# Gated edges on one Trainium2 core: sums written into the gathered rows (four buffers), loads by pairs, and a new wait before every second gather

## The reference, cut to what matters

```
concat   = [h[src], h[dst], edge_attr]            # 96 + 96 + 64 values for each edge
gates    = sigmoid(concat @ W_e + b_e)
messages = softplus(concat @ W_n + b_n)
h_new    = segment_sum(gates * messages, dst)
x        = x + h + h_new / max(edge_count, 1)
```

## Time and profile before

| | us |
|---|---|
| three runs | 3172.36, 3173.5, 3178.24 (median 3173.5) |
| the profiled execution, its own time | 3187.08 |
| its span, first to last instruction | 3185.3 |
| gated_edges within the span, about | 1266 to 2562 |

### The profile page before, as it was taken

The page is one execution under the profiler, slowest core; times in us unless marked ns, Lnnn a source line. Parts: engine busy times, 40 slices in busy tenths (PEclk is TensorE's granted clock), DMA queues, the critical chain, the costliest instruction groups (busy, mean ns, idle before and its releaser), DMA issues. The chain is left out here.

```text
span 3185.3 us, 64234 instructions
## 1 busy us (share of the span) xinstructions
PE 2435.4 (76%) x20386; PEld 2294.3 (72%) x20387; DVE 1740.3 (55%) x3596; ACT 1347.9 (42%) x2794; POOL 922.5 (29%) x1144
## 2 busy tenths in 40 slices
PE   3888889869999997665666656666566669859999
PEld 2877778759999996565566655666556557649999
DVE  7877787773444435554555445554455452345555
ACT  2544445433333332444444444444444420207776
POOL 2112111200000000566566666666666600000000
PEclk7999999979999998555555555555555559878999
DMA  2333333320000002333333333333333360028272
GB/s 67 117 101 101 104 115 103 100 77 2 2 2 2 2 2 86 95 90 91 90 91 94 91 91 89 91 93 91 90 90 91 88 244 22 1 88 348 93 259 78
DMA packets 203915, 284.20 MB, mean 89 GB/s; under 512 B 88387, under 2 KB 169542, under 8 KB 198310
## 3 DMA queue, kind: packets, MB, share of 16 engines
q1 hardware_dynamic: 164806, 201.09, 19.4%
q0 software_dynamic: 38880, 79.68, 9.6%
HBM read 211.08 MB, written 69.57 MB: 88 GB/s over the span
## 5 line engine op out<-in xcount | busy, mean ns | idle before, releaser
L1105 POOL DMA_INDIRECT layer_R<-source_terms,layer_srcs x804 | 785.4, 977 | 486.4 <-DVE layer_zp L1151 261.9
L1318 PE MATMUL layer_zp<-layer_right,layer_left 96*128 96x192 f32 x1350 | 471.7, 534 | 496.9 <-DVE layer_left L1123 472.3
L1318 PEld LDWEIGHTS layer_zp<-layer_right,layer_left 96*128 96x128 f32 x1350 | 403.3, 324 | 514.9 <-DVE layer_left L1123 474.9
L540 PE MATMUL build_win<-nodes_x,build_S 128*128 128x200 bf16 x5264 | 501.7, 252 | 126.5 <-DVE nodes_x L457 121.9
L540 PEld LDWEIGHTS build_win<-nodes_x,build_S 128*128 128x128 bf16 x5264 | 442.4, 99 | 182.0 <-DVE nodes_x L457 117.2
L910 PEld LDWEIGHTS layer_acc<-layer_U,graph_CT 128*128 128x128 f16 x6250 | 517.0, 98 | 26.5 <-issue 22.7
L910 PE MATMUL layer_acc<-layer_U,graph_CT 128*128 128x192 f16 x6250 | 521.1, 246 | 19.0 <-DVEq L759 19.0
L1151 DVE TENSOR_TENSOR layer_zp<-layer_zp,layer_R 128x1152 f32<-128x1152 f32 x135 | 184.4, 1366 | 370.7 <-remote 368.8
L1267 ACT ACTIVATE layer_y<-layer_zp 128x1152 f32<-128x1152 f32 x135 | 152.6, 1130 | 445.9 <-DVE layer_zp L1151 445.2
L1339 PEld LDWEIGHTS layer_acc<-layer_hot,layer_G 128*98 128x98 f32 x1644 | 289.0, 274 | 9.3 <-issue 3.4
L1836 PE MATMUL layer_acc<-layer_V,layer_turn 128*128 128x96 f32 x2500 | 288.6, 278 | 0.6 <-issue 0.6
(11 more groups left out here) (240 smaller groups left out, 2825.4 us busy)
## 6 DMA issues: line engine op xcount, KB each, us to landing
layer_ring<-W_blocks SPq DMA_DIRECT2D x41, 1600.0 KB, 7.7
W_blocks<-nodes_x SPq DMA_DIRECT2D x400, 100.0 KB, 1.8
layer_left<-in_attr SPq DMA_DIRECT2D x135, 192.0 KB
C_blocks<-build_Cblk SPq DMA_DIRECT2D x25, 800.0 KB, 3.6
layer_C<-C_blocks SPq DMA_DIRECT2D x25, 800.0 KB, 22.0
layer_R<-source_terms,layer_srcs POOLq DMA_INDIRECT x804
layer_rows<-target_rows SPq DMA_DIRECT2D x135, 48.0 KB
layer_right<-target_terms SPq DMA_DIRECT2D x135, 24.0 KB
```

The lines of the kernel that those rows point to most:

```text
L540: mm = pe.matmul(out, S[:, b, part, 2 * i + u, :, :].rearrange("p a z -> p (a z)"), M[:, i, u, :, :].rearrange("p a z -> p (a z)"), start= ...
L1105: nc.gpsimd.indirect_dma_start(R[:, h, u, :], None, P_d, bass.IndirectOffsetOnAxis(ap=at_u, axis=0)).then_inc(s_R[h], 16)
L1318: pe.matmul(out[u], left[:, h, u * P:(u + 1) * P], right[:, h, :], start=(u % 2 == 0), stop=False, skip_group_check=True)
```

## The change

`left`, `right`, `rows` and `R` get four buffers each (i = s % LONG); `zp`, `z`, `y`, `G` and `hot` keep two. The add writes its sum into `R[:, i]`, and the absolute value and the logs read it there. PE's product of step s then waits for the add of step s-2 in place of the logs of step s-2. The turned one-hots are made two steps ahead. SP loads for two steps at once, with one semaphore for each pair of buffers, after the product of step s-3. POOL no longer waits for the add of step s-2; it waits for the logs of step s-4 (the last readers of the buffer it fills), and in an even step also for the product of that same step. (`s_z` now begins at 4, so a count of s + 5 means that the product of step s is done.)

```
-        left = m.sb("left", [DK, 2, SE * P], F32)
-        right = m.sb("right", [DK, 2, D2], F32)
+        left = m.sb("left", [DK, LONG, SE * P], F32)
+        right = m.sb("right", [DK, LONG, D2], F32)
-        rows = m.sb("rows", [DK, 2, SE * P], I16)
-        R = m.sb("R", [P, 2, SE, D2], F32)
+        rows = m.sb("rows", [DK, LONG, SE * P], I16)
+        R = m.sb("R", [P, LONG, SE, D2], F32)
...
+            def loads(j, s):
+                two = slice(2 * j, 2 * j + 2)
+                edges = bass.ds(s * (SE * P), 2 * SE * P)
+                sp.wait_ge(s_z, s + 2)
+                sp.sem_inc(s_taken, 1)
+                sp.dma_start(rows[DE:DK, two, :].rearrange("p i e -> p (i e)"),
+                             row_d[:, edges].to_broadcast([QW, 2 * SE * P])).then_inc(s_pair[j], 16)
+                sp.dma_start(left[0:DE, two, :].rearrange("p i e -> p (i e)"), attr[:, edges]).then_inc(s_pair[j], 16)
+                for i in range(2 * j, 2 * j + 2):
+                    sp.dma_start(right[DE:DK, i, :], Q_d[bass.ds(step_base(sp, bases[i]), QW), :]).then_inc(s_pair[j], 16)
...
             for s in range(NS):
-                h = s % 2
+                i = s % LONG
                 if s == 1:
                     pool.wait_ge(s_srcs, 16)
-                pool.wait_ge(s_add, s + 1)
+                if s >= LONG - 1:
+                    pool.wait_ge(s_ms, s)
+                if s >= 2 and s % 2 == 0:
+                    pool.wait_ge(s_z, s + 5)
...
-            def turned(h, s, pair):
-                dve.wait_ge(s_rows[h], pair * 16 + 16)
+            def turned(i, s, turn):
+                if i % 2 == 0:
+                    dve.wait_ge(s_pair[i // 2], turn * 64 + 64)
...
-            def add(h, s, pair):
-                dve.wait_ge(s_R[h], (pair * 16 + 16) * SE)
-                dve.wait_ge(s_z, s + 3)
-                nc.vector.tensor_tensor(zp[h][:, :, 0:D2], zp[h][:, :, 0:D2], R[:, h, :, :], ALU.add).then_inc(s_add, 1)
+            def add(h, i, s, turn):
+                dve.wait_ge(s_R[i], (turn * 16 + 16) * SE)
+                dve.wait_ge(s_z, s + 5)
+                nc.vector.tensor_tensor(R[:, i, :, :], zp[h][:, :, 0:D2], R[:, i, :, :], ALU.add).then_inc(s_add, 1)
-            def logs(h, s):
+            def logs(h, i, s):
                 dve.wait_ge(s_l, s + 2)
-                nc.vector.scalar_tensor_tensor(z[:, h, :, D:], zp[h][:, :, D:D2], 0.0, y[:, h, :, D:],
+                nc.vector.scalar_tensor_tensor(z[:, h, :, D:], R[:, i, :, D:D2], 0.0, y[:, h, :, D:],
                                                ALU.max, ALU.add)
...
-                logs(1 - h, s - 1)
-                add(h, s, pair)
+                logs(1 - h, (i - 1) % LONG, s - 1)
+                add(h, i, s, turn)
                 if not last:
-                    turned(1 - h, s + 1, pair + h)
+                    turned((i + 2) % LONG, s + 2, turn + i // 2)
...
-                nc.scalar.activation(y[:, h, :, :], zp[h][:, :, 0:D2], ACT.Abs).then_inc(s_abs, 1)
+                nc.scalar.activation(y[:, h, :, :], R[:, i, :, :], ACT.Abs).then_inc(s_abs, 1)
...
-                pe.wait_ge(s_ms, s + 2)
-                pe.wait_ge(s_at[h], pair * 16 + 16)
+                pe.wait_ge(s_add, s + 1)
+                if i % 2 == 0:
+                    pe.wait_ge(s_pair[i // 2], turn * 64 + 64)
                 pe.wait_ge(s_hT, s + 3)
-                pe.wait_ge(s_Qs[h], pair * 16 + 16)
```

More of the change, by code:

```diff
@@ L996, in gated_edges @@
         s_init = m.sem("buffers_set")
[L997 to L1000, removed]
+        s_pair = [m.sem(f"two_steps_loaded{j}") for j in range(2)]
+        s_R = [m.sem(f"source_terms_gathered{i}") for i in range(LONG)]
         s_taken = m.sem("waits_taken")
@@ L1083, in loads @@
                         sp.dma_start(rightx[DE:DK, :], Q_d[bass.ds(past(b, v), QW), :]).then_inc(s_xQ, 16)
[L1085 to L1089, removed]
+            with sp.Fori(0, NL) as four:
+                four_steps(sp, bases, counts, four)
+                for j in range(2):
+                    loads(j, four * LONG + 2 * j)
+                    for i in range(2 * j, 2 * j + 2):
+                        more_loads(i)
         @block.gpsimd
@@ L1190, in accumulate, with step @@
                         dve.sem_inc(s_taken, 1)
-            def step(i, s, turn, pair, last):
+            def step(i, s, turn, last):
                 h = i % 2
@@ L1208, in step @@
                 onehots(h, s)
-            for words in (zp[1][:, :, 0:D2], gate, z[:, :, :, :], y[:, :, :, :], G[:, :, :, 0:D + 1], hot[:, :, :, :],
+            for words in (R[:, LONG - 1, :, :], gate, z[:, :, :, :], y[:, :, :, :], G[:, :, :, 0:D + 1], hot[:, :, :, :],
                           leftx[:, :], rightx[0:DE, :]):
@@ L1228, in _ @@
             turned(0, 0, 0)
+            turned(1, 1, 0)
             with dve.Fori(0, NS // LONG) as four:
                 for i in range(LONG):
-                    step(i, four * LONG + i, four, four * (LONG // 2) + i // 2, False)
+                    step(i, four * LONG + i, four, False)
             for s in range(NS // LONG * LONG, NS):
-                step(s % LONG, s, s // LONG, s // 2, s == NS - 1)
+                step(s % LONG, s, s // LONG, s >= NS - 2)
             gated(1, NS - 2)
-            logs(0, NS - 1)
+            logs(0, (NS - 1) % LONG, NS - 1)
             accumulate(1, NS - 2, bases[(NS - 2) % LONG], counts[(NS - 2) % LONG])
@@ L1281, in _ @@
                 for i in range(LONG):
-                    step(i % 2, four * LONG + i)
+                    step(i, four * LONG + i)
             for s in range(NS // LONG * LONG, NS):
-                step(s % 2, s)
+                step(s % LONG, s)
             gates(0, NS - 1)
@@ L1300, in _ @@
             pe.wait_ge(s_init, 1)
-            pe.wait_ge(s_wa, 80)
+            pe.wait_ge(s_wa, 144)
             pe.wait_ge(s_tab, 16)
@@ L1308, in _, with sums @@
             pe.reg_mov(more_s, 0)
-            def sums(h, s, pair, count):
+            def sums(i, s, turn, count):
+                h = i % 2
                 n = step_ranges(pe, count)
                 out = [zp[h][:, u, 0:D2] for u in range(SE)]
-                pe.wait_ge(s_ms, s + 2)
-                pe.wait_ge(s_at[h], pair * 16 + 16)
+                pe.wait_ge(s_add, s + 1)
+                if i % 2 == 0:
+                    pe.wait_ge(s_pair[i // 2], turn * 64 + 64)
                 pe.wait_ge(s_hT, s + 3)
-                pe.wait_ge(s_Qs[h], pair * 16 + 16)
                 for u in range(SE - 1):
-                    pe.matmul(out[u], left[:, h, u * P:(u + 1) * P], right[:, h, :], start=(u % 2 == 0), stop=False,
+                    pe.matmul(out[u], left[:, i, u * P:(u + 1) * P], right[:, i, :], start=(u % 2 == 0), stop=False,
                               skip_group_check=True)
@@ L1329, in sums @@
                 u = SE - 1
-                pe.matmul(out[u], left[:, h, u * P:(u + 1) * P], right[:, h, :], start=False, stop=True,
+                pe.matmul(out[u], left[:, i, u * P:(u + 1) * P], right[:, i, :], start=False, stop=True,
                           skip_group_check=True).then_inc(s_z, 1)
@@ L1348, in aggregate, with step @@
                         mm.then_inc(s_xseg, 1)
-            def step(i, s, turn, pair):
+            def step(i, s, turn):
                 if i == 0:
@@ L1353, in step @@
                     four_steps(pe, bases, counts, turn)
-                sums(i % 2, s, pair, counts[i])
+                sums(i, s, turn, counts[i])
                 aggregate(i % 2, s - 2, past_counts[i] if i < 2 else counts[i - 2])
```

51 lines of the change are left out of this document (19 added, 32 removed).

## The result

The changed kernel takes 3395.1 us (median of 4 runs, 3377.6 to 3410.4) where the kernel before takes 3172.9 in the same session: ratio 1.0697, 95% interval 1.0663 to 1.0732. It is slower, as forecast, but by 7.0% and not by 1.3%, and it lies outside the range of 3100 to 3330. The profiled execution took 3377.6, so it is compared with before's profiled 3187.08: +190.5. The four runs of the changed kernel fall into two pairs, 3378 and 3380 (granted clock 0.755 and 0.757) and twice 3410 (0.746 and 0.745); the profile is of the first pair, so what the second spends its 30 us on is not shown.

What follows compares the result with a forecast made beforehand. The prediction took a two-step cycle of waits, 18.93 us, as the bound. A 19.30 chain plus 0.1 for ports gave +0.47 x 66 = +31, plus 11 at the first stream: +42, about 3215 us, range 3100 to 3330.

Steps and rivals of the forecast that it cites:

- part 3: The new cycle: one serial chain from even gathers through add, aggregate and product to POOL, 19.30 us against 18.93, +0.37.
- The odd add: Add of step s+1: its product ends near phase 8.2, may be seen only at 17.3; off the chain.
- part 4: SP's loads for two steps at once: hidden either way; a burst beside the sixth gather delays landing at most to 9.84.
- landing: Stream start until the even step's gathered rows let its add start: taken as 9.15 us, range 8.84 to 9.84.
- GpSimd's wake-up: From the even product's end to POOL's next gather stream, on the chain: 0.27 us.
- PE's gap: Between the aggregate and the next product on PE, on the chain: 0.22 us.
- part 5: Sum moved from PSUM to SBUF: absolute value +0.03 off the chain; logs beside gathers +0.1 us, ends 0 and 1.5.
- rival C: The port pair: two logs stop POOL for their full 1.5 us inside gathers; period 20.8, 3308 us; 8%.
- A: PE truly stands still late in a stream, not only its count: period 24.1, 3528 us; 10%.
- B: The gathers' own counts are held until the stream ends: period 27.5, 3750 us; 5%.
- D: PE gets its full clock on the chain: period 16.3, 3007 us; half the cycles about 3090; 20% in all.
- The late count: Even product's completion in the kernel before is seen only 2.3 us after the last gather was issued, making its add late.

Runs made afterwards that it cites:

- z3: x1, y4 and y5 together on the changed kernel: 3211.2 us beside 3171.9, ratio 1.0121.
- x1: The changed kernel with SP starting a pair's loads after the product of step s-2 instead of s-3: 3293.5 us beside 3185.6, ratio 1.033.
- x4: The changed kernel with loads by pairs undone: four buffers stay, SP loads each step by itself after the product of step s-4: 3329.5 us, ratio 1.045.
- x2: The changed kernel with each pair's attributes loaded a second time into a spare buffer that nothing reads: 3507.9 us (one run).
- y4: x1 without GpSimd's wait for the logs at the head of a stream in even steps, leaving one wait: 3256.7 us beside 3185.4, ratio 1.0223.
- y5: x1 with PE's step table loaded before the last aggregate of a loop turn, not at the head of the next: 3253.4 us, ratio 1.0222.
- y1: x1 with PE doing the products of an odd and the next even step ahead of both aggregates: 3142.6 us beside 3185.4, ratio 0.9862.
- y7: The kernel before with three of the six gathers in each odd step, so a stream has nine: 2908.2 us (one run).
- x3: The changed kernel without POOL's wait for an even step's own product: 3275.2 us, ratio 1.028.
- z1: y1 with y4's single wait at the head of a stream: 3111.7 us beside 3171.9, ratio 0.9798.

## Why the prediction was right or wrong

**The mechanism was right** (part 3): one serial chain, POOL waiting 67 times for its product, even adds no longer at 17.3, the second stream late by 10.3 (11.4 forecast). The sign follows from it, and z3 comes back to the forecast when the costs below are taken out, though with terms that miss in both directions.

**The odd add was right by luck.** It starts at 17.4 on average (16.5 to 17.5 forecast), but not because its product is seen late: that is over at phase 5.0 and counted 0.01 later. The add waits for its own gathers. The twelfth is issued by 15.2, and the add comes 2.2 after that.

**The step that failed is part 4, loads by pairs.** It took the loads as hidden, with a landing of 9.84 at worst. The landing came at 10.76, 1.61 more than the 9.15 taken: 106 of the 154 us (66 x 2.33) that the cycles were over the forecast. Two things were wrong in it. The odd product was put at phase 8.2, so that its loads would go when the sixth gather had been issued (the 7 cycles in which they did so landed at 9.1 to 10.0); it ended near 5.0, and they went 0.7 later. And the bound of 9.84 came from the 2.3 us between the last gather and the late add of before, in a kernel whose streams have loads of one step beside them; no row bounded what 480 KB does to a landing. "Needed late, hence hidden" answers for the transfer and not for what it is beside. x1, x4 and x2 show the size: 9.40 with the burst beside the first gather, 9.96 with half of it near phase 6, 10.76 with the whole, 12.7 with the attributes doubled.

**GpSimd's wake-up** in part 3 was carried over from before at 0.27, where the instruction had one wait. The change gave it two: 0.76, +32 us (y4). Landing, wake-up and the gap below, less the ports, make up the 2.33 a cycle.

**PE's gap** in the same sum was taken as 0.22 everywhere. In every other cycle it is 1.0 more, the table's load at the head of a turn; before, the product there was not on the chain. The mean of the path from add to product is 0.33 over the forecast, and y5 takes 0.60 off it: the pieces beside the gap were put 0.27 too long, which hid part of it.

**Ports** (part 5, rival C): the effect is there, but it costs the chain next to nothing. The two logs now have two SBUF inputs. The same moment of a gather in before, and in the changed kernel:

```profile
1349.99 0.75 DVE L1157 SCALAR_TENSOR_TENSOR layer_z<-layer_zp,layer_y 128x576 f32<-128x576 f32 x1
1350.04 0.95 POOL L1105 DMA_INDIRECT layer_R<-source_terms,layer_srcs  x1 [0.30 <-issue]
```

```profile
1659.70 0.75 DVE L1159 SCALAR_TENSOR_TENSOR layer_z<-layer_R,layer_y 128x576 f32<-128x576 f32 x1
1659.73 1.54 POOL L1107 DMA_INDIRECT layer_R<-source_terms,layer_srcs  x1 [0.31 <-issue]
```

Where the second log reads PSUM the gather takes 0.95; where it reads SBUF the gather takes 1.54, that is 0.59 more for a log of 0.75. No gather beside a log takes over 0.96 in before; in the changed kernel 62 of the 81 beside L1159 take over 1.0. The rule of the Trainium skill ("SBUF — State Buffer", the section on the two separate sides) is that the one that comes second stands still until the other's instruction is over, and this trace bears it out for such a gather. It does not add up to rival C's 1.5 us a cycle, since the logs often lie partly between gathers or outside the first six, and before had a like cost from the one-hots beside the first gather (1.19). The first six gathers of a stream are 0.32 us longer than six of 0.946 now and 0.30 longer before, so the sixth is issued by phase 7.52 against 7.50. The averages, 985 and 977 ns, hide all of this.

**The other rivals.** A (PE truly stands) and B (the gathers' counts are held) are out. B: the even add starts as early as 9.0 beside a running stream. A: the product and the aggregate behind it would then be counted 1.9 us apart; the last section has 0.12. D (a faster clock on the chain) did not come, no even product ran at the full clock and the stage was granted 0.54 for 0.53; but the full clock on 12 odd products, off the chain, brought those cycles' landings 2 us forward by way of the loads.

**The late count** of before was "a rule of this trace", and no more could be said. y7 and y1's even products bear it out; x3 and y1's odd products show that counts can also come out before the stream ends. The forecast leaned on it rightly: from the new place of the product, after the stream, the count comes at once (0.01 late in all 66 even products read).

## What to carry to other kernels

A load that is early enough can still cost: write down what it is issued beside, at which phase, and what waits for that; then put it where nothing on the chain is landing. When a wait moves to another instruction, price the whole instruction, its number of waits among it, and look at what the new releaser has in front of it on its own queue: here putting the even product ahead of the two aggregates was worth 151 us (x1 to y1), and without it the four buffers only cost time. Whether that order alone would help the kernel before, with its two buffers, was not tried. An average over a group of instructions can hide a cost that moved from one to another: look at the longest ones and at what ran beside them. And rebuild a forecast that missed from its terms, one edit for each, and compare the terms too: here the total came back within 0.1%, in part because errors in both directions cancelled.

## What the runs showed of the hardware

**PE's counts are held back during a long stream of gathers.** The trace has the times at which semaphores were raised (not all of them). For PE's semaphores, the time of the count against the modelled end of the work (phase is from the first gather of the stream; medians):

```
kernel   what                  over at phase    read   count later by   count after last issue
before   odd product            4.6              65     0.01            -10.4
before   even product           9.8 to 11.1      66     6.3              +2.2
before   aggregate behind it   11.7 to 13.0      66     4.6              +2.4
y7       even product           9.8 to 11.1      66     2.1              +1.8
y1       even product          15.0 to 16.1      66     1.8              +2.2
y1       odd product            8.1 to 9.7       52     1.2              -5.1
x3       products              14.7 to 17.7      41     9.7              +3.3
x3       products               9.1 to 12.7      39    10.4              -1.8
after    even product          18.6 to 22.7      66     0.01             +5.5
```

In the cycle of the earlier trace rows the even product is counted at 1325.48 and the aggregate behind it at 1325.60. Their ends are 1.9 us apart by the profile and their counts 0.12; so the counts wait, not the work. In the same stretch counts of DVE and ACT come on time (the logs of step 3, over at 1320.43, at 1320.44). In before and y7 all counts of the even product lie within 0.25 of these medians of the last column. Elsewhere some are let out in the middle of a stream (16 of the 81 late ones in x3 over 4 us before its last issue; in z1 the one of 1558.94 at 1571.20, 1.4 before its last gather was issued; most odd products of y1, whose lateness goes from 0 to 8.9), and nearly all that fall in the first 8 us of one aren't held (43 of 45 in x3). What holds them, and what lets them out, stays open; that it needs GpSimd's gathers and not just DMA traffic wasn't tried.

**A second wait at the head of GpSimd's stream, long since met, costs 0.49 us** (0.76 against 0.27, y4 and the second stream of the changed kernel). **A burst of plain loads delays gathers in flight** by about 1.4 us on average for 480 KB (after against x1) and another 1.9 for 384 KB (x2). **A VectorE instruction with two SBUF inputs holds up the issue of a gather beside it**, here by up to 0.59 us for a log of 0.75 (the part on ports).
